# Attention maxima: causal mask added by VectorE inside the maximum instead of by mask matmuls

## The reference

```
scores = einsum('bhqd,bhkd->bhqk', q, k_h) / sqrt(HEAD_DIM)
scores = where(causal, finfo.min, scores)        # causal: k > q
attn   = softmax(scores, axis=-1)
ctx    = einsum('bhqk,bhkd->bhqd', attn, v_h)
```

## Time and profile before

| | |
|---|---|
| median of 3 runs | 2404.42 us (2399.48 to 2405.88) |
| the profiled execution's own time | 2407.62 us |
| its span | 2405.8 us |
| mean granted TensorE clock, share of full speed | 0.924 |
| TensorE busy / weight loads | 1945.4 us (81%) / 1378.8 us (57%) |
| VectorE, ScalarE, GpSimd busy | 1197.8 us (50%), 917.6 us (38%), 470.0 us (20%) |

### The profile page before, as it was taken

One profiled execution on the slowest core, in us unless ns is written; L12 is line 12 of the kernel. 1 busy time (PEld: TensorE's weight loads), 2 busy tenths in 40 slices (PEclk: granted clock), 3 DMA queues, 4 the chain that ended last, 5 costly groups with the idle time before them and its releaser, 6 DMA issues. The chain is left out here.

```text
span 2405.8 us, 39049 instructions
## 1 busy us (share of the span) xinstructions
PE 1945.4 (81%) x13768; PEld 1378.8 (57%) x13768; DVE 1197.8 (50%) x2464; ACT 917.6 (38%) x1650; POOL 470.0 (20%) x1256
## 2 busy tenths in 40 slices
PE   4888978888873989987388888888788874889988
PEld 3555655555542766765365665565556552666766
DVE  4676566565544544543444544543554444544533
ACT  3444434444431433431344433443443441433522
POOL 3221121121100211212223211231221210201201
PEclk9899989989996999998699899998999996899999
DMA  2000100100106111010200000000001005110110
GB/s 89 1 1 1 54 2 1 54 1 3 34 1 216 36 53 33 19 35 36 84 1 1 28 14 15 27 1 28 1 19 32 5 1 190 62 53 13 39 35 18
DMA packets 35322, 80.54 MB, mean 33 GB/s; under 512 B 4362, under 2 KB 5002, under 8 KB 34644
## 3 DMA queue, kind: packets, MB, share of 16 engines
q1 hardware_dynamic: 35156, 78.29, 9.8%
HBM read 61.50 MB, written 16.78 MB: 33 GB/s over the span
## 5 line engine op out<-in xcount | busy, mean ns | idle before, releaser
L245 PE MATMUL f_ring<-f_xt,f_codes 128*128 128x512 f32 (+1 forms) x1408 | 360.3, 399 | 25.0 <-DVE f_codes L1263 25.0
L245 PEld LDWEIGHTS f_ring<-f_xt,f_codes 128*128 128x128 f32 (+1 forms) x1408 | 266.0, 189 | 91.6 <-issue 26.2
L711 ACT ACTIVATE ab_region<-ab_scores 128x512 f32<-128x512 f32 x320 | 190.1, 600 | 141.7 <-PE ab_scores L891 140.8
L711 ACT ACTIVATE aa_region<-aa_scores 128x512 f32<-128x512 f32 x320 | 184.8, 598 | 128.3 <-PE aa_scores L891 124.3
L1159 POOL TENSOR_TENSOR f_ht<-f_work,f_ht 128x512 fp32r<-128x512 f32 (+1 forms) x88 | 113.4, 1293 | 580.9 <-ACT f_ht L1211 580.9
L796 DVE TENSOR_REDUCE ab_nmax<-ab_maxima 128x1 f32<-128x384 f32 (+1 forms) x256 | 149.1, 618 | 140.5 <-PE ab_maxima L891 137.9
L1284 DVE TENSOR_TENSOR f_work<-f_ring,f_work 128x512 f32<-128x512 f32 (+1 forms) x176 | 121.6, 691 | 172.2 <-ACT f_work L1200 148.2
L245 PE MATMUL f_ring<-f_dcodes,f_ht 128*128 128x512 f32 (+1 forms) x704 | 183.5, 418 | 17.6 <-DVE f_raw L1324 16.6
L890 PE MATMUL aa_maxima<-aa_stacks 96*128 96x128 bf16 (+3 forms) x512 | 144.3, 326 | 42.7 <-DVE aa_nmax L796 29.6
L1200 ACT ACTIVATE f_work<-f_ring,f_scales 128x512 f32<-128x512 f32 (+1 forms) x176 | 120.5, 685 | 144.0 <-PE f_ring L245 144.0
L245 PEld LDWEIGHTS f_ring<-f_dcodes,f_ht 128*128 128x128 f32 (+1 forms) x704 | 138.8, 200 | 57.6 <-DVE f_raw L1324 20.1
(11 more groups left out here) (185 smaller groups left out, 3657.6 us busy)
## 6 DMA issues: line engine op xcount, KB each, us to landing
f_x<-mid SPq DMA_DIRECT2D x32, 256.0 KB, 3.1
f_raw<-mid SPq DMA_DIRECT2D x32, 256.0 KB, 4.2
f_raw<-in_gate_q SPq DMA_DIRECT2D x8, 688.0 KB, 6.5
f_raw<-in_up_q SPq DMA_DIRECT2D x8, 688.0 KB, 5.6
f_raw<-in_down_q SPq DMA_DIRECT2D x10, 512.0 KB, 4.8
aa_x<-in_x SPq DMA_DIRECT2D x16, 256.0 KB, 3.1
aa_res<-in_x SPq DMA_DIRECT2D x16, 256.0 KB, 3.0
mid<-aa_res SPq DMA_DIRECT2D x16, 256.0 KB, 2.1
```

Of the source, the lines that this page charges most:

```text
L245: mm = pe.matmul(out, w, x, start=start and i == 0, stop=stop and i == len(pairs) - 1)
L711: act.activation(probs[:, s // 2 % 2, SUB * (s % 2) + i, :], scores[:, sbk, :], ACT.Exp, scale=0.25).then_inc(scores_freed[sbk].sem, 1)
```

## The change

The maxima are no longer masked by matmuls. `max_scores` issues the score matmul alone; `reduce_max` uses `tensor_tensor_reduce`, which adds a mask tile from SBUF to the scores, writes the sum back over the scores in PSUM and gives the maximum of the row as a second output. The mask tile is 512 wide, zero but for its last 128 columns, and a block of n columns takes its last n. That instruction doesn't negate, so the maximum is held with its own sign (`rowmax` in place of `nmax`) and the constant rows of the key stacks are -1 instead of 1. A semaphore increment stands between the wait and the first instruction of a block. The second pass keeps its mask matmuls.

```diff
@@ constants
-    mask_qk = ctx.enter_context(nc.sbuf_tensor("mask_qk", [P, P], BF16))
+    mask = ctx.enter_context(nc.sbuf_tensor("mask", [P, T], BF16))
...
-            pool.memset(mask_qk[:], 0.0)
+            pool.memset(mask[:], 0.0)
...
-            pool.affine_select(out=mask_qk[:], in_=mask_qk[:], compare_op=ALU.is_ge, fill=MASKED, base=0,
-                               pattern=[[-1, P]], channel_multiplier=1)
+            pool.affine_select(out=mask[:, T - P:T], in_=mask[:, T - P:T], compare_op=ALU.is_ge, fill=MASKED,
+                               base=0, pattern=[[-1, P]], channel_multiplier=1)
@@ attention
-        nmax = sb("nmax", [P, 2, NT, 2], F32)
+        rowmax = sb("rowmax", [P, 2, NT, 2], F32)
...
-        waited = sem("pool_waited")
+        waited, dve_waited = sem("pool_waited"), sem("dve_waited")
...
-            pool.memset(stacks[MAXROW:ROWS, :, HU:NST, :], 1.0).then_inc(ones_set, 1)
+            pool.memset(stacks[MAXROW:ROWS, :, HU:NST, :], -1.0).then_inc(ones_set, 1)
@@ reduce_max
-                nm, h, src = nmax[:, s % 2], k % 2, maxima[:, mb, :]
-                if k < 2:
-                    dve.tensor_reduce(nm[:, 0, h:h + 1], src[:, 0:P], AX_X, ALU.max, negate=True)
-                    last = dve.tensor_reduce(nm[:, 1, h:h + 1], src[:, P:3 * P], AX_X, ALU.max, negate=True)
-                else:
-                    qt = 1 + k // 2
-                    last = dve.tensor_reduce(nm[:, qt, h:h + 1], src[:, 0:(qt + 1) * P], AX_X, ALU.max,
-                                             negate=True)
+                nm, h, src = rowmax[:, s % 2], k % 2, maxima[:, mb, :]
+                dve.sem_inc(dve_waited, 1)
+                for qt in ((0, 1) if k < 2 else (1 + k // 2,)):
+                    n, at = (qt + 1) * P, P if qt == 1 else 0
+                    last = dve.tensor_tensor_reduce(out=src[:, at:at + n], in0=src[:, at:at + n],
+                                                    in1=mask[:, T - n:T], scale=1.0, scalar=MASKED,
+                                                    op0=ALU.add, op1=ALU.max, accum_out=nm[:, qt, h:h + 1])
                 last.then_inc(maxima_freed[mb].sem, 1)
@@ max_scores
-                    mm = block_scores(maxima[:, mb, at:at + n], st[0:STK, h, qt * P:(qt + 1) * P],
-                                      st[0:STK, hk, 0:n], mask_qk, qt * P)
+                    mm = pe.matmul(maxima[:, mb, at:at + n], st[0:STK, h, qt * P:(qt + 1) * P],
+                                   st[0:STK, hk, 0:n], start=True, stop=True)
                 mm.then_inc(maxima_filled[mb].sem, 1)
```

More of the change, by code:

```diff
@@ L150, in _ @@
                                    pattern=[[-1, P]], channel_multiplier=1)
-            pool.affine_select(out=mask_qk[:], in_=mask_qk[:], compare_op=ALU.is_ge, fill=MASKED, base=0,
-                               pattern=[[-1, P]], channel_multiplier=1)
+            pool.affine_select(out=mask[:, T - P:T], in_=mask[:, T - P:T], compare_op=ALU.is_ge, fill=MASKED,
+                               base=0, pattern=[[-1, P]], channel_multiplier=1)
             pool.affine_select(out=mask_kq[:], in_=mask_kq[:], compare_op=ALU.is_ge, fill=MASKED, base=0,
                                pattern=[[1, P]], channel_multiplier=-1)
-    return identf, identb, mask_qk, mask_kq
+    return identf, identb, mask, mask_kq
 class Norm:
@@ L361, in attention @@
               rope_dram=None, bias_dram=None, biassel_dram=None):
-    identf, identb, mask_qk, mask_kq = consts
+    identf, identb, mask, mask_kq = consts
     rope, biased = rope_dram is not None, bias_dram is not None
@@ L578, in split_max @@
             def split_max(b, s):
-                nm, nr, np_ = nmax[:, s % 2], nrest[:, s % 2], nparts[:, s % 2]
+                nm, nr, np_ = rowmax[:, s % 2], nrest[:, s % 2], nparts[:, s % 2]
                 pool.wait_ge(maxima_freed[1].sem, maxima_freed[1].at(b, MB[1] * (s + 1)))
```

## The result

The changed kernel takes **2548.4 us** (median of 4 executions, 2544.1 to 2555.8) against 2405.2 us for the kernel before, measured beside it. The ratio is 1.0595 (95% interval 1.0551 to 1.0639), so it is slower by 143 us: the side I forecast, but 28 us above the upper end of my range. The profiled executions have spans of 2405.8 and 2542.3 us, so the traces hold 136.5 us of the difference.

What follows compares the result with a forecast made beforehand. VectorE's reductions were taken to pace part of each attention step, TensorE's own work the rest. At 0.12 us added per reduction, less removed masks, +35 us in attention A and +21 in B gave 2460 us, range 2388 to 2520.

Steps and rivals of the forecast that it cites:

- TensorE isn't the bound everywhere; the removed masks give less than 59 us.: Both attentions: 1,024 removed masks give 59 us at most; counted 0.12 + 0.06 us a step in A, 0.12 + 0.17 in B.
- x = 0.12 us: Added VectorE time of each of a step's eight reductions once they have two inputs and two outputs: 0.12 us taken.
- middle case: VectorE's reductions: result costs a small queued instruction, 0.079 us added; or the overlap is lost too, 0.162 us.
- the lower end: VectorE's reductions: 128x1 result comes free, only second input and full output cost, 0.008 us added each.
- The increment: Before a block's first reduction: 0.11 us where VectorE is idle, 0.08 and 0.07 us a step; in B also 0.05.
- The sum without the clock: Both attentions, 64 steps: 5.4x - 0.10 us a step in A, 4.1x - 0.17 in B; +56 us at x = 0.12.
- The reading of the waits and the shares: Reductions delay TensorE through bank waits: 0.9 of six count in A; in B shares of 0.69, 0.2 and 0.47.
- rival 3: VectorE's reductions: nothing overlaps, x = 0.162 to 0.245, +81 to +132 us, 2485 to 2536; chance 0.22.
- Rival 1: Reductions cost what a tensor_tensor does, result free (x = 0.008): removed masks decide, -12 us, 2392; chance 0.17.
- Rival 2: Both attentions: cost and gain meet, x from 0.017 to 0.039, time 2404 us; chance 0.11.
- Rival 4: VectorE's reductions: the two-input instruction streams at half the rate, some +200 us; chance 0.03.
- What would show it: Signs: TensorE busy some 200 us less, bank waits in A over 30 us more, companions, FFNs unchanged, earlier first reduction.

Runs made afterwards that it cites:

- e1_masks_back: Changed kernel with the first-pass mask matmuls put back on TensorE, so only VectorE's half of the change is left: 2524.6 us.
- e2_masks_off: Kernel before without the first-pass mask matmuls, VectorE's instructions untouched: 2423.6 us, ratio 1.0071.
- e4_before_fill: Kernel before with eight extra mask matmuls a step in the second pass: 2415.7 us.
- e5_sem_only: Kernel before with only the semaphore increment added between the wait and the reductions of a block: 2446.6 us.
- e13_five_reductions: Kernel before with five one-column reductions a step added on VectorE, ahead of blocks k = 0, 1 and 2, no increment: 2459.2 us.
- e14_five_and_sem: Kernel before with five one-column reductions a step and the semaphore increment added: 2503.2 us.
- e15_sink_sbuf: Changed kernel with the first-pass mask matmuls put back and, in attention A alone, the sum written to SBUF instead of PSUM: 2488.7 us.
- e16_masks_back_again: Changed kernel with the first-pass mask matmuls put back, measured once more on the chip of other runs: 2523.9 us.
- e3_after_fill: Changed kernel with eight extra mask matmuls a step in the second pass: 2525.0 us.
- e8_small_op: Kernel before with a one-column memset ahead of each of the eight reductions of a step: 2428.6 us.
- e12_vector_time: Kernel before with a 40-column memset ahead of each of the eight reductions of a step: 2435.4 us.
- e9_off_and_fill: Kernel before without the first-pass mask matmuls and with each second-pass mask added twice: 2416.8 us.
- e10_off_half_fill: Kernel before without the first-pass mask matmuls and with only the second-pass masks of key tiles 0 and 2 added twice: 2412.3 us.
- e17_before_one: Kernel before with light filler: one product ahead of each block from the third on, two ahead of the row transposes: 2416.0 us.
- e18_off_hidden: Kernel before without the first-pass mask matmuls, with light filler (one product ahead of a block, two ahead of the transposes): 2422.3 us.
- e7_after_hidden: Changed kernel with four filler matmuls ahead of each block with k of 2 or more and ahead of the row transposes: 2489.2 us.
- e6_before_hidden: Kernel before with four filler matmuls ahead of each block with k of 2 or more and ahead of the row transposes: 2437.9 us.

## Why the prediction was wrong in size

**One relation holds within some 10 us for 17 of the 18 kernels.** TensorE's busy time against the kernel before is the work added or removed (matmuls of 128 columns at 0.058 us) plus about 0.4 us for each us more at 1.2 GHz:

| kernel | work | more at 1.2 GHz | work + 0.4 of it | busy, measured |
|---|---|---|---|---|
| after | -59 | +299 | +61 | +59 |
| e1_masks_back | 0 | +168 | +67 | +71 |
| e2_masks_off | -59 | +115 | -13 | -16 |
| e4_before_fill | +59 | -62 | +34 | +24 |
| e5_sem_only | 0 | +65 | +26 | +25 |
| e13_five_reductions | 0 | +71 | +28 | +30 |
| e14_five_and_sem | 0 | +122 | +49 | +50 |
| e15_sink_sbuf | 0 | +121 | +49 | +53 |
| e16_masks_back_again | 0 | +139 | +56 | +60 |
| e3_after_fill | 0 | +156 | +62 | +62 |
| e8_small_op | 0 | -7 | -3 | -3 |
| e12_vector_time | 0 | +27 | +11 | +8 |
| e9_off_and_fill | 0 | +27 | +11 | +5 |
| e10_off_half_fill | -30 | +44 | -13 | -16 |
| e17_before_one | +43 | -54 | +22 | +19 |
| e18_off_hidden | -16 | +55 | +6 | +14 |
| e7_after_hidden | +85 | -24 | +75 | +79 |
| e6_before_hidden | +145 | -109 | +101 | +68 |

The 0.4 is read off these rows, and it is what one would work out: a us at half the clock does half a us of work, so half a us is lost where TensorE works, and it works some 0.8 of the time. The one row that doesn't fit is e6_before_hidden, where the filler made TensorE busy 33 us less than that; why is open. The runs of the kernel before alone, whose code doesn't differ, show the cost too: over 64 of them, 2 x (1 - clock) x span, the time at the lower level in the whole span, has a mean of 377 us, and the span grows by 0.31 us with each us of it (correlation 0.91). The Trainium skill (TensorE: Matmul & The Clock Gate, section on HAM oscillation) counts the extra time of a throttled stretch as half of it; the batch of value products above agrees (0.60 in the mean is 0.8 of the 3.86 us at the lower level, half of that is 1.54, and it took 1.51 longer).

Point by point:

- **TensorE isn't the bound everywhere; the removed masks give less than 59 us.** Right, and the size too. From e1_masks_back to after, the removal took 59 us of work and added 26.6 us of idle, 32 us net at an equal clock; my terms for it, 0.18 us a step in A and 0.29 in B, make 0.47 x 64 = 30.
- **x = 0.12 us.** Too large: 0.043 in A. The companion exists, but the next instruction starts beside it, so neither middle case held; the measured value lies between the lower end and the lower of them. The rows of one and two inputs gave the stream rightly (0.013 us with the companion, where I had 0.008). What I had no term for is the write-back to PSUM, 0.032 us in the mean of the eight.
- **The increment.** Right as an effect on the path: 0.20 us a step is 13 us, idle rose by 11 in e5_sem_only. One costs 0.14 us on an idle VectorE, where I had 0.11. It still cost 36 us in all.
- **The sum without the clock.** My formula 64 (9.5x - 0.27) at x = 0.043 gives +9 us: 8.5 in A and 0.4 in B. Idle time +67 and work -59 give +8: in A +37 and -30, in B +30 and -30. The same terms without the masks' part give 39 us of idle for e1_masks_back (measured 40), and the masks' part alone gives -30 us for e2_masks_off (measured: idle +22, work -59, together -37). The reading of the waits and the shares held.
- **The step that failed is that sum's silence on the clock.** I priced the matmuls that stay at their duration in the trace of before. The row was before me, the 0.11 us between matmuls of 128 columns after a wait, and I put it into rival 3 as a remark without a price. It is worth 118 of the 126 us. A cure of x alone would have moved the forecast to about 2413 us, further from the result. So the right side was luck in part: what I summed comes to no more than 9 us when x is right, and it is the clock that made a clear loss of it.
- **The rivals.** Rival 3 names the right cause in one clause and the wrong one in its price (nothing overlaps). Rival 1's condition (x below 0.028) wasn't met. Rival 2's (x up to 0.039) was nearly met, and without the clock its time would have been close. Rival 4 is ruled out: the 256-wide instruction takes 465 ns where the reduction took 413.
- **What would show it.** The waits grew by more than 30 us (93.1 to 130.3 in A), the FFNs kept their length, and the companions came. Two marks failed. The first reduction was to follow the first matmul of its block sooner, and it follows 0.06 us later (0.495 to 0.557 in A). The single effects show why: without the masks it comes 0.12 us sooner (0.376 in e2_masks_off), as I had it; the increment makes it 0.14 later (0.636 in e5_sem_only); and with the new instruction it starts another 0.04 later (0.676 in e1_masks_back), for which I had nothing. TensorE's busy time was to fall by 200 us and rose by 68. The 200 was itself a slip, since neighbouring matmuls overlap: by my own 0.058 us a mask it is 59. That it rose is the mark that pointed at the missing term.

**Shown and not shown.** Shown: adding VectorE time (the five reductions; the shorter memsets made no clear change) or a sequencer step to the reductions, and taking matmuls from TensorE, each raises the time at 1.2 GHz. The means over all executions of a kernel, worked out as 2 x (1 - clock) x span against the kernel before on the same chip, agree with the single traces: +60 us for e5_sem_only, +59 for e13_five_reductions, +120 for e2_masks_off. Shown too: the lower level makes the same matmuls slower; filler takes both back in the changed kernel. Not shown: what decides in each stretch which level is granted. The ratio differs between edits: against 67, 40, 11, 21 and 39 us of added idle time (after, e1, e5, e13, e14) stand 299, 168, 65, 71 and 122 us more at the lower level, 3 to 6 for one, while e12_vector_time has 15 us more idle and 27 more at the lower level, and e8_small_op 11 and no clear change. These are single traces.

## What to carry to other kernels

Where TensorE waits briefly and often and its granted clock is already below 1, price each us of added wait at more than itself: here one us of added idle came with 3 to 6 us at the lower level in five kernels, with 2 and with none in two others, and each us at the lower level cost 0.4. Taking matmuls out of such a stage is no gain by its matmul time either; e2_masks_off saved 59 us of work and lost it to the clock and to waits. Before costing an edit by durations, look at the granted clock by stage, and if an edit makes TensorE's stream thinner, carry a term for it.

## What was unexpected of the hardware

- 59 us of matmuls removed with nothing added made the kernel 0.7% slower (1.0033 to 1.0109), and 2,500 matmuls added to the changed kernel made it 2.3% faster (2548.4 to 2489.2 us).
- A VectorE instruction with a maximum as a by-product costs up to 0.1 us more of its queue when its main output goes back to the PSUM bank than when it goes to SBUF: 0.037 us in four of the eight places of a step, 0.105 in one (0.588 and 0.483 us), nothing in three.
- The read of the accumulator is a record of 134 ns (83 behind an SBUF output) that costs some 0.01 us of the queue. The Trainium skill (VectorE: DVE Perf Modes, section on two Vector instructions with no wait between them) has the pair of instructions, which the 512 companions in each stage confirm, and no time for it.
- A semaphore increment between a wait and the instruction behind it, six a step on VectorE, costs 36 us of 2410. Each takes 0.14 us where VectorE is idle and nothing in a backlog; the rest of the 36 us is mostly TensorE's lower clock.
